# One layer pair on one core: the mask inside the bias tile, inputs normalised at once, routing in seven parts, the residual scale later, the row split on GpSimd

## The reference, cut to what matters

```python
# layer 0, attention: xi = x_norm @ down (64 channels), rmsnorm, two branches of 32 channels
def _branch(x, window, shift, ...):       # windows 10 and 20, shifts 5 and 10, 8 heads of 4
    xp = jnp.roll(pad(x), -shift, axis=1)
    qkv = (xw @ qkv_w + qkv_b)
    attn = einsum('bnqhd,bnkhd->bnhqk', q * scale, k) + bias
    attn = attn + amask                    # -100 between the two parts of the last window, 0 elsewhere
    out = einsum('bnhqk,bnkhd->bnqhd', softmax(attn), v)
# x1 = x + concat(branches) @ up ; x = x1 + gelu(rmsnorm(x1) @ w1) @ w2
# layer 0, experts: softmax router over 8, top 2, swiglu experts, and one shared expert
# layer 1: attention of 16 heads over all tokens; rmsnorm; softmax router over 8, top 2; experts with 352 hidden
```

## Time and profile before

| | us |
|---|---|
| median of 3 runs | 1742.53 (1740.51 to 1747.9) |
| the profiled execution | 1744.1 |
| its span | 1742.3 |
| busy: PE 1167.2, PE loads 630.5, DVE 1111.4, ACT 684.7, POOL 453.8 | |
| mean granted TensorE clock | 0.765 |

### The profile page before, as it was taken

One profiled execution on the slowest core, in us unless ns is written; L12 is line 12 of the kernel. 1 busy time (PEld: TensorE's weight loads), 2 busy tenths in 40 slices (PEclk: granted clock), 3 DMA queues, 4 the chain that ended last, 5 costly groups with the idle time before them and its releaser, 6 DMA issues.

```text
span 1742.3 us, 17058 instructions
## 1 busy us (share of the span) xinstructions
PE 1167.2 (67%) x5494; PEld 630.5 (36%) x5494; DVE 1111.4 (64%) x1856; ACT 684.7 (39%) x1166; POOL 453.8 (26%) x412
## 2 busy tenths in 40 slices
PE   4464665757585765532456647699997778787886
PEld 4332333434343432311122222288882323232331
DVE  3566758585857657215577586466667878677761
ACT  1112333333323333120223436443445766656663
POOL 2156611120202111243444147500003303213110
PEclk9967868777777868555556769599998888788885
DMA  8210212121221110016033124556544333253400
GB/s 281 101 59 27 71 52 67 43 83 33 83 67 58 62 40 29 6 26 81 17 56 50 18 44 98 113 169 200 200 150 74 49 45 55 41 77 45 73 20 7
DMA packets 73726, 125.03 MB, mean 72 GB/s; under 512 B 13541, under 2 KB 31014, under 8 KB 73638
## 3 DMA queue, kind: packets, MB, share of 16 engines
q1 hardware_dynamic: 65446, 107.15, 25.5%
q0 software_dynamic: 8192, 16.79, 4.0%
HBM read 57.74 MB, written 40.37 MB: 56 GB/s over the span
## 4 chain that ended last, share of the span: by engine, by line
PE 42%; DVE 23%; issue 12%; POOL 10%; ACT 8%; DMA 3%; SPq 2%; DVEq 0%; ACTq 0%; POOLq 0%
PE PS L770 5%; PE PS L813 5%; PE PS L673 5%; PE PS L623 4%; POOL XS1D L1163 4%; PE PS L790 4%; PE PS L832 4%; PE PS L573 3%; ACT P L880 3%; PE PS L750 2%; DVE MX L1553 2%; DVE WS L1307 2%; POOL YG L1147 2%; PE PS L578 2%; PE PS L736 2%
## 5 line engine op out<-in xcount | busy, mean ns | idle before, releaser
L1553 DVE TENSOR_REDUCE MX<-PS 128x1 f32<-128x512 f32 x512 | 323.8, 685 | 132.5 <-PE PS L750 123.5
L880 ACT ACTIVATE P<-PS 128x512 f32<-128x512 f32 x512 | 278.0, 596 | 194.8 <-PE PS L790 192.7
L790 PE MATMUL PS<-QS,KS 50*128 50x512 f32 x512 | 138.2, 536 | 103.6 <-ACT P L880 98.1
L750 PE MATMUL PS<-KS,QS 48*128 48x512 f32 x512 | 149.3, 580 | 66.9 <-DVE MX L1553 40.5
L770 PE MATMUL PS<-P,V 128*32 128x512 f32 x1024 | 180.3, 786 | 0.0
L1147 POOL DMA_INDIRECT A<-Y1D,POS x64 | 73.5, 1148 | 281.2 <-DMA Y1D<-YE 190.8
L750 PEld LDWEIGHTS PS<-KS,QS 48*128 48x128 f32 x512 | 58.0, 224 | 218.7 <-DVE MX L1553 112.6
L790 PEld LDWEIGHTS PS<-QS,KS 50*128 50x128 f32 x512 | 60.0, 230 | 165.5 <-ACT P L880 138.8
L623 PE MATMUL PS<-G,HEADSUM 128*128 128x400 f32 (+2 forms) x160 | 81.2, 639 | 51.5 <-DVE WS L1341 50.6
L673 PE MATMUL PS<-XST,WB 128*128 128x512 f32 x184 | 106.2, 732 | 4.4 <-issue 4.4
L813 PE MATMUL PS<-XRH,WH 128*128 128x512 f32 (+1 forms) x276 | 103.1, 414 | 0.2 <-DVE A L1495 0.2
(11 more groups left out here) (208 smaller groups left out, 2222.3 us busy)
## 6 DMA issues: line engine op xcount, KB each, us to landing
WH<-W1SD SPq DMA_DIRECT2D x23, 704.0 KB, 4.3
QS<-EH SPq DMA_DIRECT2D x64, 128.0 KB
KS<-EH SPq DMA_DIRECT2D x64, 128.0 KB
WB<-in_wb SPq DMA_DIRECT2D x23, 322.0 KB, 2.8
XS<-XS0D SPq DMA_DIRECT2D x23, 256.0 KB, 2.7
Y0D<-YE SPq DMA_DIRECT2D x23, 256.0 KB, 2.0
XS<-XS1D SPq DMA_DIRECT2D x23, 256.0 KB, 3.7
Y1D<-YE SPq DMA_DIRECT2D x23, 256.0 KB, 2.7
```

The source lines that it names most:

```text
L750: signal(pe.matmul(PS[:, s % 4, :], QS[rows, u % 3, hp, 128 * t:128 * t + 128], KS[rows, u % 3, hp, :], start=True, stop=True), "ms")
L790: signal(pe.matmul(PS[:, 4 + s % 2, :], KS[rows, u % 3, hp, 128 * k:128 * k + 128], QS[rows, u % 3, hp, :], start=True, stop=True), "st")
L880: act.activation(*a, **k).then_inc(sem[name], 1)
L1553: go("mx", dve.tensor_reduce(MX[:, u % 2, t, 4 * par + hp:4 * par + hp + 1], PS[:, s % 4, :], AX.X, ALU.max))
```

## The change

- `MASK` goes. A tile `LAST[r]` (three windows for the narrow branch, one for the wide) holds bias plus mask, filled by POOL at the start; the chunk with the last window adds it in place of the broadcast `BIAS` (L1341), and `window_max` only reduces.
- A new item `xi` replaces the norm in `window` n = 0 to 2: all 32 tiles are squared, reduced, raised to the power on POOL over 32 columns and multiplied at once. POOL then builds `BIAS` and `LAST`; DVE waits for them.
- `route` becomes seven items. In layer 0 they stand in slots 0 to 6, in layer 1 in frames 50 to 56. `trig` goes to slot 27. The prefix counts are copied out of the bank at once.
- `send(g)` goes to slot 8 + g // 2 in layer 0, and to frame 58 + g in layer 1, where POOL waits for the positions only then.
- `tail` has eight steps: the squares and POOL's power one slot earlier (4), DVE's `H` multiply in slot 6. PE's steps stay in their slots.
- DVE sums the narrow branch at n = 14 and the wide one at n = 15, each one slot later.
- The subtraction of `split` goes from DVE to POOL.

```diff
-TAIL_AT = {1: 0, 3: 1, 5: 2, 7: 3, 9: 4, 11: 5, 13: 6}
+TAIL_AT = {1: 0, 3: 1, 4: 2, 6: 3, 7: 4, 9: 5, 11: 6, 13: 7}
+ROUTE_PARTS = 7
...
-    out.append(("route",))
+    out.append(("xi",))
...
+    for n in range(ROUTE_PARTS):
+        slots[n].append(("route", n))
     for g in range(TILES):
-        slots[g].append(("send", g))
+        slots[ROUTE_PARTS + 1 + g // 2].append(("send", g))
+    slots[ROUTE_PARTS + 20].append(("trig",))
...
-    put(ROUTE_AT, ("route",))
+    for n in range(ROUTE_PARTS):
+        put(ROUTE_AT + n, ("route", n))
     for g in range(TILES):
-        put(ROUTE_AT + 2 + g, ("send", g))
+        put(ROUTE_AT + ROUTE_PARTS + 1 + g, ("send", g))
...
+            LAST = [sb0(f"LAST{r}", [128, (3, 1)[r], WIN[r], WIN[r]]) for r in range(2)]
...
             def window(b, n):
-                if n == 1:
-                    pool.wait_ge(sem["xi_sq"], b + 1)
-                    rsqrt(RSTD[:, 1], SQ[:, 0], 1.0 / 64, 1e-6, "rstd_xi")
...
+                elif what == "xi":
+                    pool.wait_ge(sem["xi_sq"], 1)
+                    rsqrt(RSTDX[:], SQX[:], 1.0 / 64, 1e-6, "rstd_xi")
                     pool.wait_ge(sem["w_b"], 16 * 18)
                     for r in range(2):
                         w = WIN[r]
                         for q in range(w):
                             ins = pool.tensor_copy(BIAS[r][:, q, :], RPB[r][:, w - 1 - q:2 * w - 1 - q])
                         go("init_p", ins)
-                    pool.wait_ge(sem["pos"], 2)
-                    pool.wait_ge(sem["zero0"], 16 * 3)
+                        last = LAST[r][:].rearrange("p w q k -> p w (q k)")
+                        go("init_p", pool.tensor_tensor(last, last, bc(BIAS[r][:].rearrange("p q k -> p (q k)"),
+                                                                       [128, (3, 1)[r], w * w], 1), ALU.add))
                 elif what == "send":
                     g = a[0]
+                    if g == 0:
+                        pool.wait_ge(sem["pos"], 2)
+                        pool.wait_ge(sem["zero0"], 16 * 3)
...
+                elif what == "split":
+                    pool.wait_ge(sem["split_hi"], a[0] + 1)
+                    go("split_lo", pool.tensor_tensor(SPL[:], STAGE[:], SPH[:].bitcast(F32), ALU.subtract))
...
             def window_max(r):
-                w, lastw = WIN[r], (PADT // WIN[r] - 1) % NWIN[r]
-                s = WS[96:128, S_AT[r] + lastw * w * w:S_AT[r] + (lastw + 1) * w * w]
-                step(dve.tensor_tensor(s, s, MASK[r][96:128].rearrange("p q k -> p (q k)"), ALU.add))
                 go(f"wmax{r}", dve.tensor_reduce(WM[r][:], window_scores(r), AX.X, ALU.max))
...
-                        bias = BIAS[r][:].rearrange("p q k -> p (q k)")
-                        go("S_sb", dve.tensor_tensor(dst, src, bc(bias, [128, m, a], 1), ALU.add))
+                        if w <= (PADT // WIN[r] - 1) % NWIN[r] < w + m:
+                            bias = LAST[r][:].rearrange("p w q k -> p w (q k)")
+                        else:
+                            bias = bc(BIAS[r][:].rearrange("p q k -> p (q k)"), [128, m, a], 1)
+                        go("S_sb", dve.tensor_tensor(dst, src, bias, ALU.add))
...
-                if n == WEXP_AT[0] + 1:
+                if n == WEXP_AT[0] + 2:
                     window_sum(b, 0)
...
-                if n == WEXP_AT[1] + 1:
+                if n == WEXP_AT[1] + 2:
                     window_sum(b, 1)
...
-                if k == 2:
+                if k == 3:
                     dve.wait_ge(sem["rstd0"], b + 1)
...
+                    sq = WS[:, 0:TILES * 64].rearrange("p (g d) -> p g d", d=64)
+                    step(dve.tensor_tensor(sq, XIR[:], XIR[:], ALU.mult))
+                    go("xi_sq", dve.tensor_reduce(SQX[:], sq, AX.X, ALU.add))
+                    dve.wait_ge(sem["rstd_xi"], 1)
+                    go("xi", dve.tensor_tensor(XIR[:], XIR[:], bc(RSTDX[:], [128, TILES, 64], 2), ALU.mult))
+                    dve.wait_ge(sem["init_p"], 5)
+                elif what == "route":
+                    route(0, RT0, 1.0 / ALPHA, *a)
+                elif what == "trig":
+                    trig()
```

More of the change, by code:

```diff
@@ L197, in turns0 @@
             uses.append(("xs", a[0]))
-        elif what == "tail" and a[1] != 2:
-            uses.append((("proj", "up", None, "h", "ffn1a", "ffn1b", "ffn2")[a[1]], a[0]))
+        elif what == "tail" and a[1] not in (2, 3):
+            uses.append((("proj", "up", None, None, "h", "ffn1a", "ffn1b", "ffn2")[a[1]], a[0]))
     return {use: n for n, use in enumerate(uses)}
@@ L1276, in route @@
-                dve.wait_ge(free, freed)
-                for k in range(2):
-                    step(dve.tensor_tensor(RT[:, 8], RT[:, 3 + k], RT[:, 7], ALU.mult))
-                    step(dve.tensor_reduce(RS[:, k], RT[:, 8], AX.X, ALU.add))
-                    go("pos" + pre, dve.tensor_copy(POS[L][:, k], RS[:, k]))
-                    dve.wait_ge(sem["pos" + pre], k + 1)
-                for k in range(2):
-                    step(dve.scalar_tensor_tensor(RT[:, 8], RT[:, 3 + k], scale, RT[:, 1], ALU.mult, ALU.mult))
-                    go("gw" + pre, dve.tensor_reduce(GW[L][:, k], RT[:, 8], AX.X, ALU.add))
-                    dve.wait_ge(sem["gw" + pre], k + 1)
+                    else:
+                        go("hot" + pre, dve.tensor_tensor(RT[:, 6], RT[:, 3], RT[:, 4], ALU.add))
@@ new lines, in route @@
+                if part == 4:
+                    ps, free = bank_filled(dve, "prefix") if L else (aux_filled(dve, "prefix"), sem["aux_free"])
+                    freed = (SHARED if L else AUX)["prefix",] + 1
+                    counts = lambda n: ps[:, TILES * E * n:TILES * E * (n + 1)].rearrange("p (t e) -> p t e", e=E)
+                    dve.wait_ge(sem["hot" + pre], 1)
+                    dve.tensor_copy(RT[:, 6], counts(0))
+                    step(dve.tensor_copy(RT[:, 7], counts(1)))
+                    dve.tensor_copy(RT[:, 5], counts(1)).then_inc(free, 1)
+                    dve.wait_ge(free, freed)
+                    at, to = 7, 8
+                    for s in (1, 2, 4, 8, 16):
+                        dve.tensor_copy(RT[:, to, 0:s], RT[:, at, 0:s])
+                        step(dve.tensor_tensor(RT[:, to, s:], RT[:, at, s:], RT[:, at, 0:TILES - s], ALU.add))
+                        at, to = to, at
@@ new lines, in route @@
+                if part == 6:
+                    for k in range(2):
+                        step(dve.tensor_tensor(RT[:, 8], RT[:, 3 + k], RT[:, 7], ALU.mult))
+                        step(dve.tensor_reduce(RS[:, k], RT[:, 8], AX.X, ALU.add))
+                        go("pos" + pre, dve.tensor_copy(POS[L][:, k], RS[:, k]))
+                        dve.wait_ge(sem["pos" + pre], k + 1)
+                    for k in range(2):
+                        step(dve.scalar_tensor_tensor(RT[:, 8], RT[:, 3 + k], scale, RT[:, 1], ALU.mult, ALU.mult))
+                        go("gw" + pre, dve.tensor_reduce(GW[L][:, k], RT[:, 8], AX.X, ALU.add))
+                        dve.wait_ge(sem["gw" + pre], k + 1)
@@ L1476, in _ @@
                     expert_out(*a)
-                elif what == "split":
-                    split(*a)
             layer0_over(dve)
```

208 lines of the change are left out of this document (95 added, 113 removed).

## The result

| | us |
|---|---|
| kernel before, same chip | 1741.52 (8 runs, 1736.35 to 1747.9) |
| changed kernel | 1754.57 (8 runs, 1752.18 to 1760.88) |
| ratio | 1.0086, 95% interval 1.0063 to 1.0109 |
| predicted | 1749, range 1728 to 1761 |

By the medians the change costs 13 us (0.75%), by the ratio 0.86%, which is 15 us (11 to 19). The forecast had 6.9. Medians from here on leave out the single runs that lay over 1.5% above the fastest of their kernel (one each of e2, e8 and r_after, two of r_spread). The profiled execution of the changed kernel took 1760.88 us (span 1759.1), 6 above its own median; that of before was 1.6 above. So stages are compared, not spans.

The account below looks back on a forecast made before the run. No engine is full; each batch is a relay where only pieces on the chain count. Layer 0 loses 11.4 us, layer 1 gains 4.5, so 6.9 more than the median of 1742.5: 1749 us, range 1728 to 1761.

Parts of the forecast that it names:

- The likeliest case: The forecast itself, send queue making DVE wait in layer 0: 1749 us, own range 1743 to 1757, chance 0.45.
- subtraction that inherits the wait: DVE's L1357 behind the maximum reduce waits for POOL's subtraction: about 3.7 us in place of 1.5.
- steady batch: Each batch after the first gains 1.55 + 0.6 + 0.6 - 0.6 = 2.15 us (bounds 0.4 to 5).
- layer 0: Send queue 22 us and trig 4.4 lost, seven batches 15 gained: 11.4 us lost.
- Mask: Two DVE mask adds go: 0.6 us and 1.55 us a batch gained, the second bounded 0 to 4.1.
- Split: Subtraction on POOL, taken as 1.5 us, delays DVE's two-input products: 0.6 us a batch lost (0.9 gained to 1.3 lost).
- Sum slot: Narrow sum one slot later: gate product fills DVE's 2.36 us idle time, wide sum starts 0.6 us earlier.
- Start: Inputs normalised at once, routing in parts: first score copy 113.8 instead of 109.23; 4.6 us lost, or 1 gained.
- Send queue: 60 sends ahead of batch 0's residual scale, ready at 207.8, hold DVE's H multiply: 22 us lost (16 to 24).
- queue hidden: Rival: sends do not stop DVE, scale is there at slot 6; about 19 us less, 1724; chance 0.18.
- Trig: Its 4.7 us of small DVE work, 0.3 hidden, moves into batch 1: 4.4 us lost.
- Layer 1: Routing in seven parts: cast's wait for embedding 9 us earlier, rows requested about 1125; 4.5 us gained (1 to 9).

Follow-up runs that it names:

- e2: Changed kernel with the split's subtraction moved back from POOL to DVE: 1747.06 us, ratio 1.0027 to the kernel before.
- e8: Changed kernel with layer 0's sends spread and the split's subtraction back on DVE, on a chip where before took 1849 us: 1809.29 us, ratio 0.9787.
- r_after: Changed kernel as it is, rerun on a third chip where the kernel before took 1834.92 us: 1835.15 us, ratio 1.0001.
- r_spread: Changed kernel with layer 0's sends spread to two or three, later one a slot, on the third chip: 1812.98 us, ratio 0.989.
- e5: Changed kernel with the two mask adds put back over zeros ahead of the maximum reduces: 1767.27 us, ratio 1.0146.
- e7: Changed kernel with routing filling DVE's waits at the start, earlier sends, split on DVE, layer 1 routing four frames earlier: 1809.1 us, ratio 0.9808 (before 1849 there).
- e3: Changed kernel with DVE's two window sums back one slot earlier, on a chip where before took 1848.64 us: 1839.25 us, ratio 0.9958.
- e1: Changed kernel with layer 0's sends spread, 22 instead of 30 send items ahead of batch 0's residual scale: 1739.76 us, ratio 0.9994.

## Why the prediction was near, and where it was off

The likeliest case was the right one: the send queue sets the result, and the steps in front of it came as summed. The size was less good. The sum came out 6 us short of the medians' difference, so the change costs nearly twice the forecast.

| step | predicted | measured |
|---|---|---|
| power over 32 columns | 6.6 | 5.43 |
| multiply, then bias tiles with both adds | 2.3 + 5.7 = 8.0 | 8.4 (75.00 to 83.41) |
| DVE free; prefix back; positions | 83; 97.0; 109.8 | 83.4; 97.5; 109.8 |
| first score copy | 113.8 | 113.6 |
| scale ready | 207.8 | 207.3 |
| subtraction that inherits the wait | 3.7 | 3.79 |
| products beside the split | 1.3 longer | 0.8 to 1.3 longer (1.3 in batch 3) |
| steady batch | 76.5 (its terms, 2.15 gained, give 76.2) | 76.0 (2.4 gained) |
| trig in batch 1 | 4.4 lost | 6.1 long |
| layer 0 | 11.4 lost | 13.4 lost |
| layer 1: cast; request for the rows | 9 and 1 gained | 9.1 and 0.2 |
| layer 1 | 4.5 gained | 4.9 at PE's first use of the rows, 4.0 at the first gather |

*Mask.* Right: the reduce ran its 1.51 us beside POOL's subtraction, and the instruction with two SBUF inputs behind it took 3.79 us and outlasted POOL's. The Trainium skill ("SBUF — State Buffer", Who interferes with whom) says just this, and e5 agrees: 2.4 us a batch where the removed adds add up to 4.65.

*Split.* Right in sign and place. On POOL it took 1.66 to 2.09 us where the sum had 1.5. e2's 7.5 us were more than the 0.6 a batch that I had; e7 and e8 agree with it.

*Sum slot.* The 0.6 is the net of e3, but of two parts, of which I had named one: the clamp behind it waits for POOL's product.

*Start.* The sum held to 0.4 us partly by luck. The power is 1.2 us cheaper, but it began at 69.51 and not at 68.4. The multiply and the bias tiles then took 8.4 us and not 8.0. That the bias tiles would stand behind DVE's multiply was right: the ten narrow copies took 3.49 us beside it, the twenty wider ones (20 elements, not ten as the prediction reads the row) 2.85 behind it, in place of 4.28 for all.

*Send queue.* Right to within a microsecond (the three pieces of POOL's work between the sends, subtraction, product and scale, start at 131.9, 158.9 and 206.0, predicted 132.4, 158.4 and 206.5), and e1 shows that it is the loss. The rival "queue hidden" failed because 60 issues at 1.26 us do fill the stretch.

*Trig.* The step "4.4 lost" was mis-sized: from 220.07 to 226.14 it takes 6.1. Its last product over 512 elements takes 2.24 in place of 0.75, since the split now runs on POOL just then:

```profile
223.90 2.24 DVE L1451 SCALAR_TENSOR_TENSOR TRIG<-TRIG,PB 128x512 f32<-128x512 f32 x1
...
223.93 1.66 POOL L1146 TENSOR_TENSOR SPL<-STAGE,SPH 128x704 fp32r<-128x704 f32 x1 [11.21 <-ACT SPH L886]
```

In e2, with the split on DVE, the same product takes 0.75. I had put both edits in the same slots and never laid one over the other. At the second projection the shift is 27.8 where my terms give 24.3: 1.7 is this, 1.8 stays open.

*Layer 1.* Right in size, and the cast's wait fell by 8.8 us as named. The rows themselves went out only 0.2 us earlier (1139.20 less the 13.4 of layer 0, against 1125.98), where I had 1. The 4.9 us come from what PE does before it: it used to reach the rows late, held up behind the cast, and now stands ready 5.38 us before they are there. So a still earlier cast would give nothing more; the last send, at 1136.96, now sets the request (SyncE waits 7.9 us for the sends to land).

*The rest.* Terms measured add up to 9.4 us at the first gather; the medians differ by 13.05. Behind it the instructions are the same, and profiles scatter there by 13 us, longer where the granted clock is lower (0.82 to 0.79). Whether the 3.6 us are scatter or a true effect, such as a lower clock that the change itself brings about, stays open.

The range held. On the third chip the answer would have been "no change", which no row of the profile before could have told.

## What to carry to other kernels

A queue that issues transfers one by one is an engine with a rate (here 1.26 us each): before moving its work later, count what must come out of it by when. Thinning out the sends was worth 15 us, as much as all the edits inside the batch gave (14.4), though its tail made DVE wait 5.97 us in another place. So count at both ends: what stands behind the queue, and what may not start until its last transfer has landed.

A wait on a shared port moves when its victim is removed: look for the next instruction that the other engine's long operation covers, and after reordering list again which instructions now fall into those spans.

Fill waits before moving work into loops: the routing parts fitted into DVE's two open waits at the start (first score copy 9.6 us earlier), and cost time in slots.

## What the runs showed of the hardware

- GpSimd's power over 32 columns took 5.43 us, over 4 columns 1.05: 0.16 us a column, 0.4 fixed.
- A one-input clamp on DVE, SBUF to SBUF in f32, is also held by a GpSimd product: 3.51 us for 0.42. The Trainium skill ("SBUF — State Buffer", Who interferes with whom) has `tensor_scalar` among those that can take the shared pair; the trace agrees. I had used only its line on two inputs.
- On two of three chips a back-to-back run of indirect transfers on GpSimd leaves PE almost still for tens of us (48 matmuls in 24.3 us in place of 2.5). The Trainium skill ("Runtime: NRT & Kernel Launch", Instruction fetch mechanics) says that each sequencer fetches its instructions in blocks over a DMA queue of its own, mostly hidden. In r_after no instruction transfer fell between 185 and 240 us, while the standstill ended at 210, so it did not end with a late block; the cause is open.
